# Splitting the layer-0 down product of odd tiles into three rounded products, with GpSimd scaling the even tiles

## What is computed

```python
coef = jnp.zeros((T, E)).at[jnp.arange(T)[:, None], topk_idx].add(topk_w)   # T tokens, E = 64 experts, 8 chosen
g = jnp.einsum('th,ehi->tei', x, Wg)                                        # h = 128, i = 64
u = jnp.einsum('th,ehi->tei', x, Wu)
h = jax.nn.silu(g) * u * coef[:, :, None]
moe_out = jnp.einsum('tei,eih->th', h, Wd)
shared = jax.nn.silu(x @ SWg) * (x @ SWu) @ SWd                             # width 128, no coefficient
x = x + attention0(xn) + moe_out + shared
...
x = x + attention1(xn) + moe1(xn)                                           # layer 1: 8 experts, the best 2 per token
```

## Time and profile before

| | before |
|---|---|
| median of 3 runs | 1770.86 us (1767.52 to 1775.95) |
| the profiled execution's own time | 1774.19 us |
| its span, first to last instruction | 1772.6 us |
| PE busy | 1693.8 us (96%) |
| DVE busy | 1324.0 us (75%) |
| ACT busy | 811.7 us (46%) |
| POOL busy | 610.3 us (34%) |
| end of the last layer-0 chunk (its last output copy starts) | 1462.5 us |

### The profile page before, as it was taken

The page is one execution under the profiler, slowest core; times in us unless marked ns, Lnnn a source line. Parts: engine busy times, 40 slices in busy tenths (PEclk is TensorE's granted clock), DMA queues, the critical chain, the costliest instruction groups (busy, mean ns, idle before and its releaser), DMA issues.

```text
span 1772.6 us, 24385 instructions
## 1 busy us (share of the span) xinstructions
PE 1693.8 (96%) x7020; PEld 1192.9 (67%) x7020; DVE 1324.0 (75%) x3818; ACT 811.7 (46%) x1457; POOL 610.3 (34%) x656
## 2 busy tenths in 40 slices
PE   6999999999999999999999999999999989888885
PEld 4677777777777777777777777777777666555553
DVE  4868788888888888888888888888888775543448
ACT  4535454545454545353535354545453535433321
POOL 4310232323232323232423232324231434555561
PEclk8999999999999999999999999999999999999998
DMA  8857555556565646464646464636363455666548
GB/s 221 187 129 215 139 151 134 156 129 161 122 167 120 170 115 175 109 181 106 184 99 173 95 177 93 176 93 176 87 173 93 114 158 181 199 194 218 169 140 305
DMA packets 172338, 273.88 MB, mean 155 GB/s; under 512 B 14312, under 2 KB 57320, under 8 KB 171952
## 3 DMA queue, kind: packets, MB, share of 16 engines
q1 hardware_dynamic: 163632, 254.63, 54.5%
q0 software_dynamic: 8576, 17.70, 3.1%
HBM read 202.15 MB, written 65.93 MB: 151 GB/s over the span
## 4 chain that ended last, share of the span: by engine, by line
PE 89%; DVE 3%; ACT 3%; another core or an unknown queue 2%; issue 2%; DMA 1%; POOL 1%; SPq 0%; ACTq 0%; DVEq 0%; POOLq 0%
PE ps_y L709 25%; PE ps_gate L662 8%; PE ps_gate L660 8%; PE ps_gate L661 8%; PE ps_up L660 7%; PE ps_up L662 7%; PE ps_up L661 7%; PE ps_y L735 3%; PE ps_side L675 3%; PE ps_side L852 1%; PE ps_side L758 1%; PE ps_side L835 1%; ACT silu_h L1317 1%; PE ps_side L794 1%
## 5 line engine op out<-in xcount | busy, mean ns | idle before, releaser
L918 DVE TENSOR_TENSOR silu_h<-ps_up,silu_h 128x512 f32<-128x512 f32 x618 | 425.4, 689 | 370.4 <-ACT silu_h L1317 263.2
L1317 ACT ACTIVATE silu_h<-ps_gate 128x512 f32<-128x512 f32 x618 | 368.0, 599 | 614.1 <-PE ps_gate L662 540.0
L709 PE MATMUL ps_y<-silu_h,w_dn 128*128 128x512 f32 x1056 | 540.5, 593 | 2.1 <-DVE silu_h L912 2.1
L912 DVE TENSOR_TENSOR silu_h<-coef_b,silu_h 128x512 f32<-128x512 f32 x528 | 388.4, 736 | 12.8 <-DMA coef_b<-coef_kept 8.5
L660 PE MATMUL ps_gate<-xnT,w_gu 128*128 128x512 f32 x528 | 340.8, 645 | 0.2 <-ACT silu_h L1317 0.2
L709 PEld LDWEIGHTS ps_y<-silu_h,w_dn 128*128 128x128 f32 x1056 | 199.5, 189 | 53.1 <-issue 7.7
L660 PE MATMUL ps_up<-xnT,w_gu 128*128 128x512 f32 x528 | 208.8, 395 | 6.6 <-DVE silu_h L918 6.6
L661 PE MATMUL ps_gate<-xnT,w_gu 128*128 128x512 f32 x528 | 209.0, 396 | 0.0
L662 PE MATMUL ps_gate<-xnT,w_gu 128*128 128x512 f32 x528 | 208.9, 396 | 0.0
L662 PE MATMUL ps_up<-xnT,w_gu 128*128 128x512 f32 x528 | 208.5, 395 | 0.0
L661 PE MATMUL ps_up<-xnT,w_gu 128*128 128x512 f32 x528 | 207.5, 393 | 0.0
(11 more groups left out here) (264 smaller groups left out, 2438.1 us busy)
## 6 DMA issues: line engine op xcount, KB each, us to landing
coef_b<-coef_kept SPq DMA_DIRECT2D x254, 512.0 KB
slots_x<-empty SPq DMA_DIRECT2D x15, 2080.0 KB, 12.6
w_block<-w_kept SPq DMA_DIRECT2D x45, 512.0 KB
xs<-slots_x SPq DMA_DIRECT2D x37, 260.0 KB
y_back<-y_kept SPq DMA_DIRECT2D x15, 512.0 KB, 7.1
w_down<-in_ffn_w SPq DMA_DIRECT2D x45, 128.0 KB
w_raw<-in_ffn_w SPq DMA_DIRECT2D x33, 128.0 KB, 4.8
xres<-in_x SPq DMA_DIRECT2D x16, 256.0 KB, 3.2
```

The costliest lines, as they stand in the source:

```text
L709: eng.matmul(ps_y[:, :], w_dn[:, j], silu_h[:, g % HBUFS], start=j == 0, stop=last).then_inc(pe_down)
L912: eng.tensor_tensor(silu_h[:, s], coef_b[:, q % COEF_RING, k], silu_h[:, s], ALU.mult).then_inc(dve_h)
L918: eng.tensor_tensor(silu_h[:, s], ps_up[g % 2][:, :], silu_h[:, s], ALU.mult).then_inc(dve_h1)
L1317: eng.activation(silu_h[:, s], ps_gate[g % 2][:, :], ACT.Silu).then_inc(act_silu)
```

## The change

Tiles with an odd number (16 of 33 in each chunk) get their down product as three float32r products. For that ScalarE rounds the finished `silu_h` tile into `h_hi` (`h_round`), GpSimd subtracts to get `h_lo` (`h_rest`), each with one buffer, and the down weights of the odd tiles are split like the gate and up weights. From the second chunk on, the coefficient of even tiles is multiplied by GpSimd (`by_pool`), not VectorE. The down product of a layer-0 tile comes four steps after its gate and up, not three (`LAG0`); "yT" and "y_add" move one step later; `silu_h` gets a fifth buffer. In the last chunk the sends of the chunk two before come one per step, at 10 to 17 (`ROUTE1_THEN`). Three loads of layer 1 wait on down products in place of up products, with smaller numbers. The scratch for the descriptors of GpSimd's DMAs is cut to 2048 bytes.

```diff
-DOWN_PART = 11
+DOWN_PART = 8
-LAG = 3
-TILES_UNDER_XS, TILES_UNDER_XST, TILES_UNDER_WEIGHTS = 9, 15, 27
-HBUFS = 4
+LAG0, LAG1 = 4, 3
+TILES_UNDER_XS, TILES_UNDER_XST, TILES_UNDER_WEIGHTS = 8, 12, 22
+HBUFS = 5
+HI_BUFS, LO_BUFS, SPLIT_LATE = 1, 1, 3
-FINISH0 = [(3, "yT"), (4, "y_add")]
+FINISH0 = [(4, "yT"), (5, "y_add")]
+ROUTE1_THEN = [(at, what) for at, what in ROUTE1 if not what.startswith("send")] + [(43 + n, f"send{n}") for n in range(TOP1 * ROWS)]
-        plan[g] += [(what, c - 2) for at, what in ROUTE1 if at == j + TILES0 and c > 1]
+        plan[g] += [(what, c - 2) for at, what in (ROUTE1 if c < SPARSE else ROUTE1_THEN) if at == j + TILES0 and c > 1]
...
-        w_raw = sb("w_raw", [STAGES_W, 2, P], within=early)
+        w_raw = sb("w_raw", [STAGES_W, 3, P], within=early)
-        w_gu = sb("w_gu", [TILES0, 2, 2, P], FP32R, within=ffn0)
-        w_dn = sb("w_dn", [TILES0, P], within=ffn0)
+        w_two = sb("w_two", [PAIRS0 // 2, 5 * 2, P], FP32R, within=ffn0)
+        w_last = sb("w_last", [2 * 2, P], FP32R, within=ffn0)
+        w_dn = sb("w_dn", [PAIRS0 // 2 + 1, P], within=ffn0)
+        h_hi = sb("h_hi", [HI_BUFS, CHUNK], FP32R, within=ffn0)
+        h_lo = sb("h_lo", [LO_BUFS, CHUNK], FP32R, within=ffn0)
...
+        def by_pool(g):
+
+            return TILES0 <= g < TILES and scaled(g) and not odd(g)
...
             def last_products(g):
...
+                if odd(g):
+                    n, w = odd_before(g), weights0(j)[:, 2]
+                    hi, lo = h_hi[:, n % HI_BUFS], h_lo[:, n % LO_BUFS]
+                    eng.wait_ge(act_hhi, n + 1)
+                    eng.matmul(ps_y[:, :], w[:, 0], hi, start=False, stop=False)
+                    eng.matmul(ps_y[:, :], w[:, 1], hi, start=False, stop=False)
+                    eng.wait_ge(pool_hlo, n + 1)
+                    eng.matmul(ps_y[:, :], w[:, 0], lo, start=False, stop=False).then_inc(pe_down)
+                    return
...
 +            def h_round(g):
+                n = odd_before(g)
+                eng.wait_ge(dve_h, dve_before(g) + 1)
+                if n >= HI_BUFS:
+                    eng.wait_ge(pe_down, odd_at(n - HI_BUFS) + 1)
+                eng.copy(h_hi[:, n % HI_BUFS], silu_h[:, g % HBUFS]).then_inc(act_hhi)
...
+                if odd(g - SPLIT_LATE):
+                    h_round(g - SPLIT_LATE)
                 if TILES_FIRST <= g < TILES + UNITS1:
                     silu(g)
...
 +            def times_coef(g):
+                s = g % HBUFS
+                eng.wait_ge(dve_h1, g + 1)
+                q, k = wait_coef(eng, g, g % TILES0 % COEF_TILES == 0)
+                eng.tensor_tensor(silu_h[:, s], coef_b[:, q % COEF_RING, k], silu_h[:, s], ALU.mult).then_inc(pool_h)
+
+            def h_rest(g):
+                n = odd_before(g)
+                eng.wait_ge(act_hhi, n + 1)
+                if n >= LO_BUFS:
+                    eng.wait_ge(pe_down, odd_at(n - LO_BUFS) + 1)
+                eng.tensor_tensor(h_lo[:, n % LO_BUFS], silu_h[:, g % HBUFS], f32(h_hi[:, n % HI_BUFS]), ALU.subtract).then_inc(pool_hlo)
...
             for g in range(STEPS):
+                if odd(g - SPLIT_LATE):
+                    h_rest(g - SPLIT_LATE)
+                if by_pool(g - 1):
+                    times_coef(g - 1)
                 for what, key in plan[g]:
                     step(what, key, g)
...
-    nc = bacc.Bacc("TRN2", target_bir_lowering=False, num_devices=1)
+    nc = bacc.Bacc("TRN2", target_bir_lowering=False, num_devices=1, dynamic_dma_scratch_size=2048)
```

More of the change, by code:

```diff
@@ L427, in scaled_before, with odd, odd_before, odd_at @@
             return c * PAIRS0 + j
+        def odd(g):
+            return 0 <= g < TILES and g % TILES0 % 2 == 1
+        def odd_before(g):
+            c, j = tile_of(g)
+            return c * (PAIRS0 // 2) + j // 2
+        def odd_at(n):
+            c, k = divmod(n, PAIRS0 // 2)
+            return c * TILES0 + 2 * k + 1
+        def by_pool(g):
+            return TILES0 <= g < TILES and scaled(g) and not odd(g)
+        def pool_coefs_before(g):
+            c, j = tile_of(g)
+            return max(c - 1, 0) * (PAIRS0 // 2) + (j + 1) // 2 if c > 0 else 0
+        def dve_before(g):
+            return scaled_before(g) - pool_coefs_before(g) if g < TILES else scaled_before(g) - (CHUNKS - 1) * (PAIRS0 // 2)
+        def wait_coef(eng, g, wait):
+            q, k = divmod(scaled_before(g), COEF_TILES)
+            if q == 0:
+                eng.wait_ge(coef_first[k], 2 * 16)
+            elif wait:
+                eng.wait_ge(coef_in[q % COEF_RING], 2 * 16 * (q // COEF_RING + (q % COEF_RING > 0)))
+            return q, k
+        def weights0(j):
+            if j == TILES0 - 1:
+                parts = w_last[:, :, :]
+            else:
+                parts = w_two[:, j // 2, 4:10] if j % 2 else w_two[:, j // 2, 0:4]
+            return parts.rearrange("p (a b) d -> p a b d", b=2)
+        def raw_of(n):
+            return w_raw[:, n % STAGES_W, 0:2 + n % 2]
         def dense(g):
@@ L679, in first_products @@
                 c, j = tile_of(g)
-                gu = w_gu[:, j]
+                gu = weights0(j)
                 eng.wait_ge(*read("xT0", c))
```

70 lines of the change are left out of this document (38 added, 32 removed).

## The result

The change made the kernel slower: 1883.9 us (median of 4 runs, 1880.51 to 1890.58) against 1769.19 (1766.69 to 1775.95) for the kernel before. The ratio is 1.0642, with a 95% interval of 1.0619 to 1.0665. The sign was forecast; the size was not (+46 forecast, +115 measured, outside the range).

What follows compares the result with a forecast made beforehand. TensorE alone was taken to set layer 0's pace; 43 us saved by odd products, outweighed by waits on GpSimd's late subtractions, summed to +46 us, so 1817 us forecast, with 8 in 10 for 1750 to 1857.

Steps and rivals of the forecast that it cites:

- The product of three: Odd tile's down product as three float32r products 0.23 us apart: saves 0.17 us per tile, 2.7 per chunk, 43 in all.
- Step 7: Chunks 1 to 15, tile 3: TensorE waits 1.8 us because GpSimd's subtraction stands behind "stats1".
- Step 13: Tile 9: its subtraction on GpSimd, behind query work and send0, comes late; TensorE waits 1.2 us.
- Steps 15 to 19, weight parts: Subtractions of tiles 11, 13, 15 late behind sends: 1.6 us; two weight parts add 1.7 in chunks 2 to 9.
- I count no wait there: Second half of a chunk: only three message sums and prefix counts on GpSimd, so no TensorE wait was counted.
- VectorE loses 240 x 0.69 us and nobody waits for it: Middle chunks: the coefficient products taken off VectorE give nothing there, neither gain nor loss.
- the message sums: Three GpSimd operations in the second half of a chunk, for which no wait was counted.
- My waits are of the shorter kind, so nothing: Clock rival: products slow from 0.40 to 0.63 us behind a longer wait in the last chunk; put at nothing.
- the two elementwise engines block each other: Rival: shared SBUF port lock delays VectorE, late for up banks by perhaps 3 us a chunk; 1859 us, chance 0.09.
- Sum by stage: Chunk 0 -2.7, chunk 1 -0.9, chunks 2 to 9 +29, 10 to 14 +9.5, 15 +10, start +1: +46 us.
- GpSimd's price: Each new coefficient product or subtraction on GpSimd takes 1.40 us, ends 1.27 and 1.62; POOL busy near 1300 us.
- for the whole instruction: In the blocking rival: exclusive port lock held by a two-SBUF-input VectorE instruction against a GpSimd instruction that reads SBUF.

Runs made afterwards that it cites:

- kernels without reads: Changed kernel with GpSimd's added operations as fills that read nothing: ratio 1.0264; also stats1 and two scatters later 0.9807; instead two buffers, one step earlier, scatters later 0.9765.
- the changed one with fills: Changed kernel with GpSimd's two added operations replaced by fills that write the same buffers and read nothing; ratio 1.0264 to the kernel before.

## Why the prediction was wrong in size

**Right.** *The product of three:* in the changed kernel its three parts start at 1008.44, 1008.67 and 1008.89 and the next product at 1009.12, 0.23 apart. The kernels without reads and nearly without waits save 2.2 to 3.0 us in a middle chunk (2.7 forecast). *Step 7:* forecast 1.8; the wait there is 1.7 with TensorE's restart, and moving "stats1" gave back 26.4 us. *Step 13:* forecast 1.2; the wait is 1.2 in the same count, and the step's own distance grew by 1.02. *Steps 15 to 19, weight parts:* for steps 0 to 19, less the saving of ten odd products, I had +4.6 with weight parts and +2.9 without; 4.2 and 2.3 were measured. The sum fits better than its parts: in chunks 10 to 14 step 19 grew by 0.6 to 0.7 us where I had a wait of 1.1, less 0.17.

**The step that failed** is the sentence "I count no wait there" on the second half of a chunk, and with it "VectorE loses 240 x 0.69 us and nobody waits for it". Forecast for steps 20 to 32 was -1.0 us (six odd products); measured were +3.1 to +5.5. Over chunks 1 to 14 these halves took 55 us more where I had 14 less: 69 us, as much as the whole miss. I had listed GpSimd's own work there and found little. I hadn't asked what its new operations do to VectorE's old ones. The delays reach TensorE as waits for the banks of up at steps 20, 22 and 23 (0.34, 0.65 and 1.98 us in the chunk from 1174.07 us on; step 23 alone is 2.1 us longer than before). And once, at step 31, TensorE waits for h_lo (1.04 us). There a second thing failed that I had called harmless, the message sums, in the same chunk:

```profile
1264.11 1.75 POOL L1655 TENSOR_TENSOR msg<-msg 128x512 f32<-128x512 f32 x1
1265.82 1.26 POOL L1668 TENSOR_TENSOR h_lo<-silu_h,h_hi 128x512 fp32r<-128x512 f32 x1
```

The third message sum takes 1.75 us and stands right ahead of the subtraction. What moving it would give back was not tried.

**A term put at nothing** that was not nothing is the clock: "My waits are of the shorter kind, so nothing". The clock fell in six of chunks 2 to 14, behind waits of up to 2 us that followed one another, and in the last one. This is worth at most 13 us by the estimate above, and by the chunks' lengths some 0.7 us in each of the six.

**The rival that had the mechanism** was "the two elementwise engines block each other", at 0.09 and 1859 us. Its price was too low for two reasons that the runs show. I counted every held operation at 0.7 us; the dearest, one by one, were small ones, 2.3 us extra on a product of 128x128, since GpSimd's two operations stand back to back in a step and VectorE's waits for both. (In total the coefficient products weigh as much: 0.42 us more on each of 132, 56 us between 400 and 1200 us.) And I spread its cost over the chunk, while it falls where VectorE's routing and attention products meet steps that are due. By the kernels without reads it is worth about 67 us in the change as it stands, and about 110 once there is room, the clock's share included in both.

**Sum by stage**, in us over before, forecast and measured: first copy -2 and +7.2; chunk 1 -0.9 and +3.3; chunks 2 to 9 +29 and +61.9; chunks 10 to 14 +9.5 and +37.0; chunk 15 +10 and +7.1. Chunk 0 was missed as well: in 30 to 125 us PE now waits 6.0 us for VectorE's `silu_h` and 3.2 for `h_lo` (2.6 and nothing before). What exactly is late in it was not tried.

**A smaller term** that I didn't have: what the list calls a wait is less than what it costs. In the changed kernel L769 starts at 1213.17 and L771 at 1214.46, 1.29 us apart instead of 0.23, and the next product 0.34 behind instead of 0.23; the list says 0.90. Each wait costs 0.16 + 0.11 = 0.27 us more than its number, about 25 us over the 93 waits listed.

**GpSimd's price** was nearly right, 1.33 and 1.32 instead of 1.40, and POOL is busy 1243 us instead of some 1300.

## What to carry to other kernels

Work that is moved to GpSimd can be paid for twice: by its place in GpSimd's queue, and by every two-SBUF-input instruction of VectorE that meets it and has something due behind it; look through VectorE's small instructions in those steps, since a tiny one waits as long as a large one. Ask of each moved piece when it is due, not how full its engine is: GpSimd at 53% was harmless, at 60% ruinous and at 67% a gain, by which tiles were chosen. A wait of TensorE can be paid for a second time, by a lower clock behind it, so look at the clock in short stretches. A saving that is the same for every tile should be taken on those tiles whose chain has room, and left on the others.

## What the runs showed of the hardware

A VectorE instruction with two SBUF inputs waited not for one GpSimd instruction but for all that followed without a gap: 3.35 us for a product that takes 0.28, through two operations. In the rows above it was already held from 456.13, while the indirect DMA's span was still running on GpSimd and the next operation began only at 456.80; L1023 before it passed untouched in the same span. Whether that is the rough end of GpSimd's spans or a claim made ahead of the operation isn't settled. The prediction has the lock held "for the whole instruction"; the section it cites of the Trainium skill, "SBUF — State Buffer", says this of VectorE's modes with two ports, and here the wait went on past one GpSimd instruction.

Not only products of two inputs were held. A small operation with one input, between 400 and 1200 us, before and in the change:

```profile
L1178 DVE TENSOR_SCALAR top_neg<-best 128x4 f32<-128x4 f32 x9 | 1.5, 162 | 0.0
L1243 DVE TENSOR_SCALAR top_neg<-best 128x4 f32<-128x4 f32 x8 | 5.9, 736 | 0.0
```

The landing of a scatter that frees a row buffer is no constant. From the start of send3's issue to the end of the wait for it, 2.4 to 3.1 us passed before (once 4.7), and 5.7 to 6.4 in chunks 2 to 14 of the kernel with rounding and subtraction one step earlier. In one and the same kernel, the changed one with fills, it was 5.3 to 5.9 in chunks 2 to 9, which have the weight parts, and 2.7 to 2.9 in chunks 10 to 14. What makes it longer was not tried. Kernels that change layer 0's output also scatter to other rows.
